# A two-layer vision tower on one core: normalisations, residuals and the feed-forward in halves of the tokens, and the routing cut into more steps

## The reference, cut to what matters

```python
h = tok_embed(x)                                   # x @ W + position table
h = h + attn0(layernorm(h))                        # group norm, 8 heads of 64, its own residual inside
h = h + ffn0(layernorm(h))                         # gelu(tril(W1) x + b1), then tril(W2), over the channels
h = h + attn1(layernorm(h))                        # 8 heads of 16
h = h + switch_ffn(layernorm(h))                   # softmax over 16 experts, top 1, capacity by running count
```

## Time and profile before

| | |
|---|---|
| median of 3 runs | 6809.92 us (6809.24 to 6820.73) |
| the profiled execution's own time | 6804.59 us |
| its span, first to last instruction | 6802.8 us |
| mean granted clock of TensorE | 0.951 |
| busy: PE, DVE, ACT, POOL | 89%, 66%, 47%, 37% |

### The profile page before, as it was taken

The page is one execution under the profiler, slowest core; times in us unless marked ns, Lnnn a source line. Parts: engine busy times, 40 slices in busy tenths (PEclk is TensorE's granted clock), DMA queues, the critical chain, the costliest instruction groups (busy, mean ns, idle before and its releaser), DMA issues.

```text
span 6802.8 us, 126677 instructions
## 1 busy us (share of the span) xinstructions
PE 6049.1 (89%) x40167; PEld 4017.5 (59%) x40167; DVE 4474.2 (66%) x11034; ACT 3218.6 (47%) x6321; POOL 2516.2 (37%) x2135
## 2 busy tenths in 40 slices
PE   6788898998989889898998989989898998989986
PEld 4556665665656666565665656666565665656543
DVE  4456676776757667576776767767676676767664
ACT  2345545444444444554544444454544544454531
POOL 3534433433333333333433333343333433333300
PEclk7899999999999999999999999999999999999987
DMA  2121221221122121211212222121211212222110
GB/s 59 41 67 41 58 51 29 63 51 46 46 53 49 39 52 42 59 42 38 63 42 49 49 50 49 44 50 45 59 42 38 63 34 57 49 50 44 25 30 9
DMA packets 98046, 317.01 MB, mean 47 GB/s; under 512 B 27782, under 2 KB 32854, under 8 KB 87126
## 3 DMA queue, kind: packets, MB, share of 16 engines
q1 hardware_dynamic: 97366, 308.41, 19.6%
HBM read 57.19 MB, written 41.94 MB: 15 GB/s over the span
## 4 chain that ended last, share of the span: by engine, by line
issue 44%; POOL 25%; PE 22%; DVE 4%; ACT 2%; DMA 2%; SPq 1%; POOLq 1%; DVEq 0%; ACTq 0%
POOL pr_lo L506 21%; PE bank L884 4%; PE bank L912 3%; PE bank L945 3%; POOL on L1265 2%; PE bank L910 2%; PE bank L870 2%; PE bank L929 2%; PE bank L930 2%; DMA stacks<-parts 1%; DVE mxh L1630 1%; PE bank L719 1%; PE bank L818 1%; PE bank L708 1%; PE bank L955 1%
## 5 line engine op out<-in xcount | busy, mean ns | idle before, releaser
L1630 DVE TENSOR_REDUCE mxh<-bank 128x1 f32<-128x512 f32 x4096 | 2789.0, 688 | 1797.3 <-PE bank L884 1779.6
L1143 ACT ACTIVATE pr<-bank 128x512 f32<-128x512 f32 x4096 | 2418.4, 598 | 2723.7 <-PE bank L912 2679.9
L884 PE MATMUL bank<-stacks 128*128 128x512 f32 x4096 | 2221.3, 543 | 348.4 <-DVE mxh L1630 233.9
L506 POOL TENSOR_TENSOR pr_lo<-pr 128x1024 bf16<-128x1024 f32 x1024 | 1944.7, 1902 | 911.4 <-ACT pr L1143 909.1
L912 PE MATMUL bank<-stacks 65*128 65x512 f32 (+1 forms) x4096 | 1673.2, 409 | 27.7 <-ACT pr L1143 27.7
L884 PEld LDWEIGHTS bank<-stacks 128*128 128x128 f32 x4096 | 799.9, 195 | 1090.2 <-DVE mxh L1630 757.7
L929 PE MATMUL bank<-v,pr 128*128 128x129 bf16 x8192 | 1063.5, 222 | 94.6 <-POOL pr_lo L506 93.3
L930 PE MATMUL bank<-v,pr_lo 128*128 128x129 bf16 x8192 | 1051.1, 220 | 0.0
L929 PEld LDWEIGHTS bank<-v,pr 128*128 128x128 bf16 x8192 | 779.5, 98 | 393.1 <-issue 346.3
L1265 POOL TENSOR_TENSOR on<-on,o_r 128x128 f32<-128x128 f32 x512 | 205.4, 401 | 2045.5 <-DVE on L1660 2045.4
L912 PEld LDWEIGHTS bank<-stacks 65*128 65x128 f32 (+1 forms) x4096 | 800.2, 195 | 261.4 <-ACT pr L1143 94.4
(11 more groups left out here) (170 smaller groups left out, 4925.2 us busy)
## 6 DMA issues: line engine op xcount, KB each, us to landing
stacks<-parts SPq DMA_DIRECT2D x384, 512.0 KB, 6.5
stacks<-parts_d SPq DMA_DIRECT2D x224, 128.0 KB, 3.0
parts_d<-mx SPq DMA_DIRECT2D x16, 1024.0 KB, 4.5
stacks<-parts_d SPq DMA_DIRECT2D x224, 64.0 KB, 2.8
stage<-in_pe SPq DMA_DIRECT2D x16, 512.0 KB, 7.8
stacks<-mrow SPq DMA_DIRECT2D x512, 2.0 KB
parts_d<-on SPq DMA_DIRECT2D x16, 512.0 KB, 5.2
parts_d<-stage SPq DMA_DIRECT2D x16, 512.0 KB, 6.2
```

Source lines behind the costliest of these rows:

```text
L506: return eng.tensor_tensor(low_of(u, kt - 1).rearrange("p a b -> p (a b)"), w, hi, ALU.subtract)
L884: mm(maxb[k % 2][:, :], qs[:, t * P:(t + 1) * P], ks[:, g * HALF:(g + 1) * HALF], start=True, stop=True).then_inc(max_filled.sem, 1)
L1143: act.activation(pr[:, at % 2, kt, :], score[k % 2][:, :], ACT.Exp, scale=SCALES[layer]).then_inc(exp_done.sem, 1)
L1630: dve.tensor_reduce(mxh[:, layer, n // 2, n % 2:n % 2 + 1], maxb[k % 2][:, :], AX_X, ALU.max)\
```

## The change

Every normalisation, `residual1`, and the whole chain of the feed-forward are done by halves, each with its own semaphore counts and its own slots. The routing is cut at more steps. The core of the diff:

```diff
-    at = {"copy": -40, "oT0.3.0": -34, "attn0.0": -30, "oT0.3.1": -23, "attn0.1": -21, "ln1": -20, "z1": -18, "zT1.0": -13,
-          "zT1.1": -12, "ffn_h0": -10, "ffn_h1": -9, "ffn_o0": -7, "ffn_o1": -6, "ln2": -5, "z2": -3}
+    halves = ({"oT0.3": -34, "attn0": -30, "ln1": -28, "z1": -26, "zT1": -23, "ffn_h": -21, "ffn_o": -18, "ln2": -16, "z2": -14},
+              {"oT0.3": -23, "attn0": -21, "ln1": -19, "z1": -17, "zT1": -14, "ffn_h": -12, "ffn_o": -9, "ln2": -7, "z2": -5})
+    return {"copy": LAST[kind] - 40, "res0": LAST[kind] - 13, **slots}
...
-    at = {"xT0": 179, "xT1": 180, "h0": 182, "h1": 183, "ln": 184, "z": 187, "zT0.0": 190, "zT0.1": 191, "gn": 192,
+    at = {"xT0": 179, "xT1": 180, "h0": 182, "h1": 184, "ln.0": 184, "ln.1": 186, "z.0": 187, "z.1": 188, "zT0.0": 190, "zT0.1": 191, "gn": 192,
...
-        at = {"oT1.0": 18, "oT1.1": 19, "attn1.0": 21, "attn1.1": 22, "ln": 24, "z": 27, "zT3.0": 31, "zT3.1": 32,
+        at = {"oT1.0": 18, "oT1.1": 19, "attn1.0": 21, "attn1.1": 23, "ln.0": 23, "ln.1": 25, "z.0": 26, "z.1": 28, "zT3.0": 30, "zT3.1": 32,
...
     # POOL, rstd of one half
-                    pool.wait_ge(stats_ready[n].sem, stats_ready[n].at(b, 1))
-                    var, dst, eps, width = mv[:, s, :, 1], rs[:, s, :], pool_c[:, 1, :], T
+                    pool.wait_ge(stats_ready[n].sem, stats_ready[n].at(b, g + 1))
+                    var, dst, eps, width = mv[:, s, ts, 1], rs[:, s, ts], pool_c[:, 1, 0:4], 4
...
     # POOL, feed-forward: one generator for each half, and the two residuals apart
+            def mlp(seg, g):
+                yield AT[f"ln1.{g}"]
+                rstd(seg, seg.l0, 1, g=g)
+                yield AT[f"z1.{g}"]
+                residual1(seg.l0, g)
+                yield AT[f"ln2.{g}"]
+                rstd(seg, seg.l0, 2, g=g)
+            def residuals(seg):
+                yield AT["copy"]
+                    copy_hm(seg)
+                yield AT["res0"]
+                    residual0(seg, seg.nxt)
...
     # DVE, embedding
-                    yield AT[f"h{g}"]
+                    yield AT[f"h{g}"] + 1
                     add_result(seg, f"{pre}h{g}", g, stage, stage)
-                yield AT["ln"]
-                norm_stats(seg, 0, stage)
-                yield AT["z"]
-                norm_apply(b, 0, stage)
+                    yield AT[f"ln.{g}"] + 1
+                    await_drained(dve, seg, f"{pre}h{g}")
+                    norm_stats(seg, 0, stage, g)
+                for g in range(2):
+                    yield AT[f"z.{g}"]
+                    norm_apply(b, 0, stage, g)
...
     # DVE, switch: the same with attn1.g, then the routing
+                yield AT["logits"] + 1
+                yield AT["route"] + 1
                 link(seg, dve.reciprocal(rp, total))
+                yield AT["rank"] + 1
                 bank, drained = await_filled(dve, seg, f"{pre}rank")
+                yield AT["place"] + 1
                 for t in range(T):
+                    if t % 4 == 0:
+                        yield AT["place"] + 2 + t // 4
                     ins = dve.scalar_tensor_tensor(hm[:, t, :], z[:, t, :], un[:, t:t + 1], hm[:, t, :], ALU.mult, ALU.add)
```

More of the change, by code:

```diff
@@ L209, in switch_slots @@
     return {**at, **{f"e{n}.{d}": s + d for n, s in enumerate(first) for d in range(2)}}
-NO_BANK = ("ln", "z", "route", "place", "copy", "ln1", "z1", "ln2", "z2", "gn", "xn")
+NO_BANK = ("route", "place", "copy", "res0", "gn", "xn", *(f"{name}.{g}" for name in ("ln", "z", "ln1", "z1", "ln2", "z2") for g in range(2)))
 def glue_plan(kind):
@@ new lines, in mlp @@
+                yield AT[f"oT0.3.{g}"]
+                heads_turn(seg, 3, g)
+                yield AT[f"attn0.{g}"]
+                bank, filled = use(seg, f"attn0.{g}", *(f"oT0.{c}.{g}" for c in range(NCH)))
+                for j in range(4):
+                    t = 4 * g + j
+                    for c in range(NCH):
+                        last = mm(bank[:, j * P:(j + 1) * P], heads_T(c)[:, t * P:(t + 1) * P], wo_sb[:, c, :],
+                                  start=(c == 0), stop=(c == NCH - 1))
@@ new lines, in mlp @@
+                last.then_inc(filled, 1)
+                yield AT[f"zT1.{g}"]
+                z_turn(seg, seg.l0, 1, g)
+                yield AT[f"ffn_h.{g}"]
+                bank, filled = use(seg, f"ffn_h.{g}", f"zT1.{g}")
+                mm(bank[:, :], w1T[:, :], zT[:, g * HALF:(g + 1) * HALF], start=True, stop=True).then_inc(filled, 1)
+                yield AT[f"ffn_o.{g}"]
+                bank, filled = use(seg, f"ffn_o.{g}", f"ffn_h.{g}")
+                for j in range(4):
+                    t = 4 * g + j
+                    last = mm(bank[:, j * P:(j + 1) * P], gelu_s[:, t * P:(t + 1) * P], w2T[:, :], start=True, stop=True)
@@ L1002, in segment @@
                 if seg.l0:
-                    beside += [Beside(more_heads(seg)), Beside(more_values(seg)), Beside(done_heads(seg)), Beside(mlp(seg))]
+                    beside += [Beside(more_heads(seg)), Beside(more_values(seg)), Beside(done_heads(seg)), *(Beside(mlp(seg, g)) for g in range(2))]
                 if seg.nxt:
@@ L1333, in segment @@
                 if seg.kind == "first":
-                    rstd(seg, seg.l0, 0)
+                    for g in range(2):
+                        rstd(seg, seg.l0, 0, g=g)
                     residual0(seg, seg.l0)
                     rstd(seg, seg.l0, 4, "a.")
-                beside = [Beside(mlp(seg))] if seg.l0 else []
+                beside = [Beside(residuals(seg)), *(Beside(mlp(seg, g)) for g in range(2))] if seg.l0 else []
                 if seg.nxt:
@@ L1703, in segment @@
                 if seg.l0:
-                    beside += [Beside(more_heads(seg)), Beside(more_values(seg)), Beside(mlp(seg))]
+                    beside += [Beside(more_heads(seg)), Beside(more_values(seg)), *(Beside(mlp(seg, g)) for g in range(2))]
                 if seg.nxt:
```

183 lines of the change are left out of this document (74 added, 109 removed).

## The result

The changed kernel takes **6845.7 us** (median of 5 runs, 6843.1 to 6854.2), the kernel before beside it 6810.1 us (5 runs, 6809.2 to 6820.7). The ratio is 1.005, with a 95% interval of 1.0035 to 1.0065: slower by 36 us, where 6780 us had been forecast, 30 us faster. Even the range (6735 to 6832) misses it.

The account below looks back on a forecast made before the run. PE, busy 89% of the span, was taken to set the time. Terms of -1.2 us a round over 13 rounds (-15) plus the other segments (-15) gave -30 us: 6780 us, range 6735 to 6832.

Parts of the forecast that it names:

- What bounds the kernel: Whole span: PE, busy 89%, sets the time; the change can move only the 11% standing and the half-clock stretches.
- Feed-forward, -4.5: Feed-forward, per round: 8.5 us idle removed, 5.2 added, 1.2 from the clock; -4.5 us, bounds -8 and -2.
- the collision: Feed-forward, steps 242 to 245: GpSimd's `residual0` blocks VectorE's application z2.0, so PE stands 3.2 us.
- no collision: Feed-forward's lower bound: `residual0` does not block z2.0; -8 us a round.
- Embedding, +2.2: Embedding, per round: three waits summing to 7.7 us replace one stall of 5.5; +2.2 us, bounds -0.1 to +3.4.
- the second wait: Embedding, step 185: e15.1 waits for VectorE to drain h1's bank behind a reduction, half statistics and addition; 2.3 us.
- the third: Embedding, tile 190: PE waits for the reduction of 188 behind statistics, applications and expert accumulations; 4.3 us.
- Switch, +0.3: Switch, per round: PE stands about 3.4 us at step 26 for the low part, other stalls go; net +0.3 us.
- Routing, +0.85: Routing, per round: running count drained a step later, so POOL's low parts and PE's 2.14 us stall follow; +0.85 us.
- Other segments, -15: Outside the 13 rounds: second segment -5, penult -4.5, first segment's tail and last switch -5.6 us.
- The slower rival: Embedding and switch: POOL's low parts catch the halves' applications; +8 to +35 us, middle 6830; chance 0.22.
- seven signs of being right: Profile signs: waits at L870, L740, L929; L1425 over 1 us; less idle before L806, L912, L884.

Follow-up runs that it names:

- the three orders put right: Changed kernel with the rank's prefix back in its own step, GpSimd's next-sequence residual later, and its switch reciprocal roots behind the low part: 6729.5 us.
- the run with busy matmuls: Kernel before plus 22 matmuls of no use on PE in the 5.5 us wait ahead of step 190's maximum tile: 6825.7 us, ratio 1.0030.
- the rank's cut: Kernel before with only the rank's prefix a step later on VectorE: +49 us.

## Why the prediction was wrong

By its own steps:

- **What bounds the kernel.** Right that PE sets the time. The step that failed is the sentence that a change which leaves PE's work alone "can only move the 11% in which PE stands still and the stretches at half clock", of which it then priced the first and took the second as given, but for 2.4 us taken back in the feed-forward (-1.2 us in the sum). The clock is a term of its own: 11.6 us more at 1.2 GHz, +5.8 us a round.
- **Feed-forward, -4.5.** Right in the changed kernel: -4.5 over steps 224 to 256, the collision and its stall (3.2 forecast, 2.9 measured) included. Alone it was -3.5 there and only -1.5 in the round, by the clock behind it. The lower bound for "no collision", -8, was too far: without it the stretch gives -6.1 in its own steps.
- **Embedding, +2.2.** Right in size (+2.4) by luck, wrong in its terms: the second wait was 1.7 us and not 2.3, the third 1.6 and not 4.3, so that PE stands 0.3 us less in steps 176 to 208; 4.6 us more at 1.2 GHz there, 3.5 of them in steps 184 to 192, took their place.
- **Switch, +0.3.** The mis-sized term. Stall and place are as forecast (3.3 us at step 26), and the stalls of 0.9 and 2.0 us went as forecast; the steps 24 to 40 cost +1.5, because each round now has 3.4 us at 1.2 GHz behind it.
- **Routing, +0.85.** The other one: the stall grew by 0.9 us exactly as said, and steps 48 to 64 cost +3.5, since they have 4.1 us more at 1.2 GHz. "The other cuts cost nothing" missed a stall of 0.9 us at step 55.
- **Other segments, -15.** First segment +4.8 from its first scores (what lies ahead of them took 2.2 less), second -5.3 (forecast -5), penult +1.5 (-4.5), last -2.8. The penult's -5.5 was not the sum of its terms either: the feed-forward's -4.5 without the collision's 3.2 is -7.7. With the three orders put right the first is -3.1 and the penult -2.3. What of POOL's order held the first segment was not separated.
- **Rivals.** The slower rival came nearest (+8 to +35, measured +36), but by the wrong mechanism and place: applications were not all caught by low parts, the embedding lost 2.4 us and not 3.4 to 5.5, and the largest loss of a round, +3.5, is in the routing, of which it said nothing new. It was given 22 in 100. That a stall may be longer-lived than itself, by the clock, was in no case.

Of the forecast's -1.2 us a round, standing time was about 0 (2.2 - 3.3 + 0.3 + 0.85) and the clock -1.2; in the trace they are -2.3 and +5.8. Six of its seven signs of being right came true, only L870's wait was 1.7 us and not over 2: the idle time before L806 in the whole span went from 21.2 us to nothing, and that of the maximum tile by DVE from 14.2 to 10.7 in the fifth round. All of them are signs of standing time, and so could not tell this outcome. The prediction read the queues well and forgot what PE does after a wait.

## What to carry to other kernels

Price a stall of TensorE as its length plus half of the time at 1.2 GHz that the trace shows behind stalls of that kind; the page gives both sums at once, span less busy PE and twice what the mean clock lacks to 1. When work is cut into halves, look at every queue (here GpSimd's) in which a half now waits for something ahead of work that TensorE needs: here three lines, two of GpSimd and one of VectorE for which GpSimd waits, decided between 0.5% slower and 1.1% faster. A stall cut into three with little between them can cost more than the whole one.

## What was not expected of the hardware

- **The same stall is followed by the low clock in one kernel and not in the other.** The stall of 2.0 us at step 29 is in the kernel before followed by 3.4 us at 1.2 GHz in 1 round of 13, in the run with busy matmuls in every round; that at step 201 (2.0 us) in at most 5 rounds of 12 in most kernels, and in 9 to 11 of 12 in four of them. The parts' costs do not add: alone their standing times sum to -3.6 us a round and their time at 1.2 GHz to +18.3, together they are -2.3 and +11.6; the medians sum to +80 us, together they make +36. The Trainium skill (TensorE: Matmul & The Clock Gate, section Part 1: The HAM clock gate) says that the clock follows how busy TensorE has lately been; the two runs with matmuls put into the stalls agree. Why an unchanged stall changes sides is not settled.
- **The rounds' lengths bunch.** In the kernel before the loop's rounds take 406.1 to 412.4 us, 8 of 13 between 409.4 and 410.2; in the changed one 409.9 to 415.8, 7 between 412.9 and 413.3; with the rank's cut, 7 lie between 413.0 and 413.5. With that cut a stall 0.9 us longer goes with a mean round 3.4 us longer. It was not tried what sets this.
- **A new wait at the start of a round.** In the run with 22 more matmuls a round at step 190, 1.35 us of standing time with nothing that the profile can name (1.40 in the row above) came to the round's first steps, at an instruction that no part of the edit touched. The length of PE's list alone doesn't make it: the run with 23 more a round at steps 26 and 50 has none there. The cause was not sought.
